# One block for setup and first attention of a two-layer decoder, with the loads and small products reordered

## What is computed

```python
q = (query @ w_q + b_q); k = (query @ w_k + b_k); v = (query @ w_v + b_v)     # 256 -> 16 * 128 each
weights = softmax(q k^T / sqrt(128), causal)
out = (weights @ v) @ w_o + b_o
Q, K = h @ Wq.T, h @ Wk.T                      # h is the context, 64 -> 64, 4 heads
sim = sum_heads(Q K^T) / 16                    # 256 x 256 per batch
threshold = 76th largest of each row of sim    # then sigmoid, mask, symmetric mean
```

## Time and profile before

| what | before |
|---|---|
| median of 3 runs, us | 876.88 (874.26 to 877.98) |
| the profiled execution, us | 877.31 |
| its span, us | 875.5 |
| TensorE busy | 793.7 us, 91% |
| VectorE, ScalarE, GpSimd busy | 65%, 48%, 57% |
| granted clock of TensorE, mean | 0.967 |

### The profile page before, as it was taken

One profiled execution on the slowest core, in us unless ns is written; L12 is line 12 of the kernel. 1 busy time (PEld: TensorE's weight loads), 2 busy tenths in 40 slices (PEclk: granted clock), 3 DMA queues, 4 the chain that ended last, 5 costly groups with the idle time before them and its releaser, 6 DMA issues. The chain is left out here.

```text
span 875.5 us, 14612 instructions
## 1 busy us (share of the span) xinstructions
PE 793.7 (91%) x4733; PEld 680.5 (78%) x4733; DVE 572.2 (65%) x1659; ACT 422.3 (48%) x1193; POOL 500.1 (57%) x409
## 2 busy tenths in 40 slices
PE   7889999999999976594899989999987799999995
PEld 5678888888988865293688878988885488888884
DVE  4696967868668576323678968777737655554555
ACT  5264635536346556061366654666663633323232
POOL 4857187566668451603475565367422386777763
PEclk9999999999999998797999999999999799999998
DMA  6220702204215211554210110110001011111111
GB/s 206 73 97 1 241 19 78 97 6 140 85 61 175 92 55 34 172 144 101 61 48 31 55 55 7 50 55 25 25 1 38 13 45 46 54 36 54 40 38 48
DMA packets 58331, 59.09 MB, mean 67 GB/s; under 512 B 5392, under 2 KB 49312, under 8 KB 58272
## 3 DMA queue, kind: packets, MB, share of 16 engines
q1 hardware_dynamic: 57504, 56.24, 20.7%
q0 software_dynamic: 768, 2.10, 0.7%
HBM read 50.00 MB, written 8.32 MB: 67 GB/s over the span
## 5 line engine op out<-in xcount | busy, mean ns | idle before, releaser
L981 ACT ACTIVATE a_probs<-bank,a_neg_peak 128x128 f32<-128x128 f32 (+1 forms) x256 | 103.5, 428 | 105.7 <-DVE a_neg_peak L1099 105.7
L1099 DVE CUSTOM_DVE_ANT_0 bank<-bank,causal 128x128 f32<-128x128 f32 (+1 forms) x256 | 82.7, 393 | 33.4 <-PE bank L842 32.1
L1009 ACT ACTIVATE a_probs<-a_probs,a_row_inv 128x128 f32<-128x128 f32 (+1 forms) x256 | 92.0, 454 | 8.3 <-DVE a_row_inv L1107 8.3
L987 ACT ACTIVATE a_probs_t<-bank 128x512 f32<-128x512 f32 x96 | 54.1, 600 | 62.3 <-PE bank L862 62.3
L881 PE MATMUL bank<-a_probs_t,a_vals 128*128 128x256 f32 x256 | 77.8, 386 | 3.3 <-DVE a_ot_lo L1119 3.3
L1821 POOL TENSOR_TENSOR d_h_lo<-d_h,d_h_hi 128x512 fp32r<-128x512 f32 x40 | 51.7, 1293 | 45.5 <-ACT d_h_hi L1941 31.9
L693 POOL TENSOR_TENSOR a_queries<-sim 128x512 f32<-128x512 f32 x32 | 41.1, 1283 | 62.2 <-DVE sim L1074 62.2
L2027 DVE TENSOR_TENSOR d_h<-d_silu,bank 128x512 f32<-128x512 f32 x40 | 27.5, 689 | 71.8 <-PE bank L128 70.5
L126 PE MATMUL bank<-a_wo_hi,a_ot_hi 128*128 128x256 f32 x256 | 73.0, 285 | 1.0 <-issue 1.0
L128 PE MATMUL bank<-a_wo_hi,a_ot_lo 128*128 128x256 f32 x256 | 72.0, 281 | 0.0
L127 PE MATMUL bank<-a_wo_lo,a_ot_hi 128*128 128x256 f32 x256 | 71.9, 281 | 0.0
(11 more groups left out here) (328 smaller groups left out, 2416.6 us busy)
## 6 DMA issues: line engine op xcount, KB each, us to landing
d_raw<-in_L_ffn_we_dram SPq DMA_DIRECT2D x48, 128.0 KB, 2.2
raw_k<-in_L_attn_w_k_dram SPq DMA_DIRECT2D x8, 512.0 KB, 6.8
raw_q<-in_L_attn_w_q_dram SPq DMA_DIRECT2D x8, 512.0 KB, 5.9
raw_v<-in_L_attn_w_v_dram SPq DMA_DIRECT2D x8, 512.0 KB, 7.9
raw_o<-in_L_attn_w_o_dram SPq DMA_DIRECT2D x8, 512.0 KB, 3.6
kv<-_L_ffn_expert_masks_dram SPq DMA_DIRECT2D x16, 256.0 KB, 3.0
kvt<-_L_ffn_expert_masks_dram SPq DMA_DIRECT2D x16, 256.0 KB, 3.2
raw_o<-in_L_attn_Wo_dram SPq DMA_DIRECT2D x8, 512.0 KB, 3.6
```

What stands on the lines that cost most here:

```text
L981: nc.scalar.activation(probs[s % 2][:, i, at:at + width], c.banks[i][:, at:at + width], ACT.Exp, bias=neg_peak[:, n:n + 1], scale=-1.0, ac ...
L987: nc.scalar.activation(probs_t[:, i * BANK:(i + 1) * BANK], c.banks[3 + (3 * s + i) % 2][:], ACT.Copy).then_inc(s_pt_free, 1)
L1009: last = nc.scalar.activation(part, part, ACT.Copy, scale=row_inv[:, s % 2, n + r:n + r + 1])
L1099: last = nc.vector.tensor_tensor_reduce(part, part, mask, -1.0, 3e38, ALU.add, ALU.min, neg_peak[:, n + r:n + r + 1])
```

## The change

`setup` goes, and a class `Beginning` takes its place; its parts are called from inside layer 0's attention block, so that there is one block in place of two. Raw keys and queries are loaded right after the first half of x, then biases, context, small weights, router, the second half of x, values. TensorE transposes the first half of x, runs four more warming matmuls into bank 7, transposes the biases, projects keys of step 0 (with a semaphore of their own, `s_split_k`), then transposes the context, small weights and the second half of x, projects the queries, and makes the context products and graph scores; the columns' products follow the scores of step 0. The doubled copies go from GpSimd to VectorE. Context and graph buffers live in buffers used later. GpSimd adds the output bias inside step 0, after the split of the second values; the wait for it at line 1194 goes, and one is written under `if rope and s == PASS_STEPS - 2`. What is not shown of the diff: the new semaphores and small buffers, and the copies and subtractions for high and low parts, which are those of before with their own semaphores.

```diff
...
-        with AttentionWeights(c, 0) as weights:
-            setup(c, weights)
-            attention(c, 0, weights)
+        with AttentionWeights(c, 0) as weights, Beginning(c) as beginning:
+            attention(c, 0, weights, beginning)
...
-def setup(c, weights):
...
+class Beginning:
...
+        self.ctx_nat = c.spare[:, 0].rearrange("p (t a d) -> p t a d", t=NT, a=2)
+        self.ctxt_hi, self.ctxt_lo, self.kt_hi, self.kt_lo = c.kvt_hi, c.kvt_lo, c.kvg_hi, c.kvg_lo
+        self.qt = c.kv_hi[:].rearrange("p t n -> p (t n)")
...
+    def loads(self, sp, weights):
+        c, a = self.c, self.a
+        sp.dma_start(c.ident[:], a["ident"]).then_inc(self.s_const, 16)
+        self.load_x(sp, 0)
+        for n in "kq":
+            weights.load(sp, n, 0)
+        for i, n in enumerate(("b_q", "b_k", "b_v")):
+            sp.dma_start(self.bias_nat[i * HEADS:(i + 1) * HEADS], a[f"L0_attn_{n}"].rearrange("(h d) -> h d", d=DH)).then_inc(self.s_bias, 16)
+        sp.dma_start(self.ctx_nat[:, :, 0], a["ctx_512"].rearrange("b (t p) d -> p (b t) d", p=P)).then_inc(self.s_ctx, 16)
+        for i, n in enumerate(("L0_xattn_Wq", "L0_xattn_Wk", "L1_xattn_W_k")):
+            sp.dma_start(self.w_nat[:, i, 0], a[n]).then_inc(self.s_w, 16)
+        sp.dma_start(self.r_nat[:], a["L0_ffn_router_w"]).then_inc(self.s_router, 16)
+        self.load_x(sp, 1)
+        weights.load(sp, "v", 0)
+        sp.dma_start(self.causal_f[:], a["causal"]).then_inc(self.s_mask, 16)
+        sp.dma_start(self.g_raw[:], a["L0_xattn_gamma_raw"].partition_broadcast(P)).then_inc(self.s_mask, 16)
+        sp.dma_start(c.rows[:, ROW_BK, 0:DC], a["L1_xattn_b_k"].partition_broadcast(P)).then_inc(self.s_key_bias, 16)
+        sp.dma_start(c.rows[:, ROW_BK, DC:P], a["L1_xattn_b_k"].partition_broadcast(P)).then_inc(self.s_key_bias, 16)
+        weights.load(sp, "o", 0)
+        sp.dma_start(c.ffn_weight[:], a["L0_ffn_weight"].rearrange("(k p) i -> p k i", p=P)).then_inc(c.s_ffn_weight, 16)
+        for r, n in ((ROW_BO, "L0_attn_b_o"), (ROW_SCALE, "L0_ffn_scale"), (ROW_GAMMA, "L1_xattn_ln_gamma"), (ROW_BETA, "L1_xattn_ln_beta")):
+            sp.dma_start(c.rows[:, r], a[n].partition_broadcast(P)).then_inc(c.s_rows, 16)
+    def load_x(self, sp, h):
+        sp.dma_start(self.c.x[:, 4 * h:4 * h + 4], self.a["x"][2 * h:2 * h + 2].rearrange("b (t p) d -> p (b t) d", p=P)).then_inc(self.s_x[h], 16)
+    def turn_x(self, pe, h):
+        c = self.c
+        pe.wait_ge(self.s_x[h], 16)
+        for k in range(KC):
+            for t in range(4):
+                last = self.nc.tensor.transpose(c.banks[3 + k][:, t * P:(t + 1) * P], c.x[:, 4 * h + t, k * P:(k + 1) * P], c.ident[:])
+            last.then_inc(self.s_x_t, 1)
+    def turn_first(self, pe):
+        c, nc = self.c, self.nc
+        pe.wait_ge(self.s_idle, 1)
+        keep_warm(c, 9)
+        pe.wait_ge(self.s_const, 16)
+        self.turn_x(pe, 0)
+        keep_warm(c, 4, 7)
+        pe.wait_ge(self.s_bias, 3 * 16)
+        nc.tensor.transpose(c.banks[2][:, 192:192 + 3 * HEADS], self.bias_nat[:], c.ident[0:3 * HEADS, 0:3 * HEADS]).then_inc(self.s_bias_t, 1)
+        pe.wait_ge(self.s_x_lo, KC)
+    def turn_others(self, pe):
+        c, nc = self.c, self.nc
+        pe.wait_ge(self.s_twice, 1)
+        for h in range(2):
+            for t in range(4):
+                last = nc.tensor.transpose(c.banks[h][:, t * P:(t + 1) * P], self.ctx_nat[:, 4 * h + t].rearrange("p a d -> p (a d)"), c.ident[:])
+            last.then_inc(self.s_ctx_t, 1)
+        pe.wait_ge(self.s_twice, 2)
+        pe.wait_ge(self.s_biased, 1)
+        for i in range(3):
+            nc.tensor.transpose(c.banks[2][:, i * DC:(i + 1) * DC], self.w_nat[:, i].rearrange("p a d -> p (a d)"), c.ident[0:DC, 0:DC])
+        pe.wait_ge(self.s_router, 16)
+        for k in range(KC):
+            last = nc.tensor.transpose(c.banks[2][:, 256 + k * EXPERTS0:256 + (k + 1) * EXPERTS0], self.r_nat[:, k * P:(k + 1) * P],
+                                       c.ident[0:EXPERTS0, 0:EXPERTS0])
+        last.then_inc(self.s_small_t, 1)
+        self.turn_x(pe, 1)
...
+    def products(self, pe):
+        c, nc = self.c, self.nc
+        pe.wait_ge(self.s_small_lo, 1)
+        pe.wait_ge(self.s_ctx_lo, 2)
+        for n in range(4):
+            if n == 3:
+                pe.wait_ge(self.s_x_lo, 2 * KC)
...
+        for h in range(2):
+            if h:
+                pe.wait_ge(self.s_qk_lo, 1)
...
+            last.then_inc(self.s_rows, 1)
+        pe.wait_ge(self.s_qk_lo, 4)
+        for b in range(B):
+            if b == 3:
+                pe.wait_ge(self.s_kv, 1)
...
+            last.then_inc(self.s_scores, 1)
+        pe.wait_ge(self.s_kv, 2)
+        pe.wait_ge(self.s_sim, 2)
+    def columns(self, pe):
+        for h in range(2):
+            pe.wait_ge(self.s_sim, 3 + h)
+            mm_stacked(self.nc, self.c.banks[3 + h][:], self.weight(2), self.ctxt_hi[:, cols], self.ctxt_lo[:, cols], False).then_inc(self.s_columns, 1)
...
+    def high(self, act):
+        c, nc = self.c, self.nc
+        self.high_x(act, 0)
+        act.wait_ge(self.s_bias_t, 1)
...
+        self.high_x(act, 1)
+        nc.scalar.activation(c.ident_bf[:], c.ident[:], ACT.Copy)
+        act.wait_ge(self.s_mask, 32)
+        nc.scalar.activation(c.causal[:, 1], self.causal_f[:], ACT.Copy)
+        nc.scalar.activation(self.g_exp[:], self.g_raw[:], ACT.Exp, scale=-1.0).then_inc(self.s_gamma, 1)
+        for n in range(4):
+            act.wait_ge(self.s_qk, n + 1)
+            nc.scalar.activation((self.qt, self.kt_hi)[n // 2][:, self.half(n % 2)], c.banks[n][:], ACT.Copy).then_inc(self.s_qk_hi, 1)
+        for b in range(B):
...
+    def low_first(self, dve):
+        c, nc = self.c, self.nc
...
+        self.low_x(dve, 0)
+        dve.wait_ge(self.s_ctx, 16)
+        nc.vector.tensor_copy(self.ctx_nat[:, :, 1], self.ctx_nat[:, :, 0]).then_inc(self.s_twice, 1)
+        dve.wait_ge(self.s_w, 3 * 16)
+        nc.vector.tensor_copy(self.w_nat[:, :, 1], self.w_nat[:, :, 0]).then_inc(self.s_twice, 1)
+        dve.wait_ge(self.s_biased, 1)
+    def low_others(self, dve):
+        c, nc = self.c, self.nc
+        for h in range(2):
+            dve.wait_ge(self.s_ctx_hi, h + 1)
...
+        dve.wait_ge(self.s_small_hi, 1)
...
+        self.low_x(dve, 1)
...
+    def gamma(self, dve):
+        c, nc = self.c, self.nc
+        dve.wait_ge(self.s_gamma, 1)
...
+        dve.wait_ge(self.s_sim, B)
+    def splits(self, pool, weights):
+        self.nc.gpsimd.memset(self.c.half_neg[:], -0.5)
+        self.nc.gpsimd.memset(self.c.one[:], 1.0)
+        pool.drain()
+        weights.first_splits(pool)
...
@@ -457,7 +512,7 @@
         parts = []
         for n, heads in (("k", min(self.KH, 2)), ("q", 2)):
-            if parts and self.rope:
+            if parts and (self.rope or s == 0):
                 self.split(pool, parts, self.s_split_k)
                 parts = []
...
@@ -646,6 +701,8 @@
                 if rope:
                     weights.load(sp, "q", 1)
                     weights.load(sp, "k", 1)
+                else:
+                    beginning.loads(sp, weights)
...
@@ -744,14 +801,12 @@
                 if rope:
                     rotate(0)
                 else:
+                    beginning.splits(pool, weights)
                     split_v(0)
                 split_proj(2)
                 if rope:
                     rotate(1)
                     weights.gather(pool, 1)
-                else:
-                    pool.wait_ge(c.s_rows, 4 * 16)
-                    nc.gpsimd.tensor_tensor(c.x[:], c.x[:], c.rows[:, ROW_BO].unsqueeze(1).broadcast_to([P, NT, D]), ALU.add).then_inc(s_residual, 1)
                 for s in range(LAST + 1):
                     if not rope and s % STEPS:
                         split_o(s // STEPS)
@@ -765,6 +820,9 @@
                         split_o(s // STEPS)
                     if s % STEPS == 0 and s < LAST - 1 and not rope:
                         split_v(s // STEPS + 1)
+                    if not rope and s == 0:
+                        pool.wait_ge(c.s_rows, 4 * 16)
+                        nc.gpsimd.tensor_tensor(c.x[:], c.x[:], c.rows[:, ROW_BO].unsqueeze(1).broadcast_to([P, NT, D]), ALU.add).then_inc(s_residual, 1)
                     if rope and s == NORM_STEP - 1:
                         weights.root(pool, 1)
                     if not rope and s % STEPS and s // STEPS < 4:
@@ -792,6 +850,8 @@
                         what, j = units(s)[u]
                         if rope and what == "k":
                             pe.wait_ge(weights.s_split_k, group_of(s, what) + 1)
+                        elif what == "k" and s == 0:
+                            pe.wait_ge(weights.s_split_k, 1)
                         else:
                             pe.wait_ge(s_split_proj, s + 1)
                         bank = claim("proj", s, u)
...
-                proj(0, range(len(units(0))))
                 if rope:
```

(25 more changed lines are left out.)

285 lines of the change are left out of this document (102 added, 183 removed).

## The result

| what | before | after |
|---|---|---|
| median of 11 runs each, us | 877.45 (874.26 to 880.3) | 871.45 (867.87 to 874.15) |
| the profiled execution, its span | 877.31, 875.5 | 867.87, 866.0 |
| granted clock, mean | 0.967 | 0.970 |

The ratio is 0.993, 95% interval 0.9912 to 0.9947: 6.0 us faster, 0.7% (4.7 to 7.7 us by the interval). The forecast was 870.3 with 867.5 to 874.5. It went by a median of 876.88 for before, from three runs; over eleven it is 877.45.

A forecast was written before the change was run, and what follows sets the result against it. TensorE, busy without a gap from 66 to 290 us, was taken as the bound, so gains lay ahead of it: 4.3 us in the front plus 2.3 in the search, 6.6 off, giving 870.3 us (range 867.5 to 874.5).

The forecast's parts named there:

- Part 1: Start of the front: with reordered loads, keys land at 6.7 us, biases at 8.9, and TensorE's first projection starts at 9.3.
- Part 2: First projection to step 1: 17.6 us of work plus 0.3 wait, step 1 at 27.2 against 31.47, 4.3 us won.
- Part 3: Top-k search: copy of sim no longer held by GpSimd's addition, first values at 33.1 us, 6.6 us won by then.
- Late and colliding (B): Rival, chance 0.15: late keys, longer graph-score wait, addition colliding with VectorE's search end or next copy; 3.3 us won, 873.6.
- Part 4: After the search: moved addition delays no loads, step 4's split ready about 65 us with 14 us slack, new wait costs nothing.
- The sum: Whole kernel: 4.3 + 2.3 = 6.6 us off, giving 870.3 us in terms of the median of before.
- A: Rival, chance 0.2: TensorE's clock falls in the wait before the keys, first projections lose 1.4 us; 5.2 won, 871.7.
- C: Rival, chance 0.1: the front was covered, something unseen takes the gain back after 290 us; 876 to 877.
- D: Rival, chance 0.05: pauses between small pieces keep TensorE at 1.2 GHz from 9.3 us until step 1; 11 us slower, 887.9.

## Why the prediction was right

- **Part 1** held. The first projection came at 9.67 against 9.3. Keys landed at 7.1 instead of 6.7 and the biases at 9.3 instead of 8.9; the clock stayed up behind the wait for the biases in both profiles of after (1.86 and 2.50 us).
- **Part 2** held: 17.70 us from there to step 1 against 17.6 + 0.3. The wait of the graph scores was 0.23 us. Together 4.1 us won against 4.3. That took the clock at 1.00 from 9.67 on, as the profiles of after show it; nothing says in how many of the eleven executions it was so.
- **Part 3** held, but for one line. First values 32.96 (33.1), search end 43.28 (43.5), 6.80 us earlier against 6.6. What it rests on, the addition holding the copy, is now shown by taking the copy away in before: 2.58 us. The line that failed is that GpSimd has nothing in flight at the first copy: its split of queries was (29.22 to 30.52), and the copy took 0.96 us instead of 0.3. That cost nothing, as the search's later operations waited for ScalarE's copy of the values in the run without the copy (0.85 us, up to 35.32) and came at the same time in after (35.34). The Trainium skill, "SBUF — State Buffer", section "Who interferes with whom", says that a VectorE instruction with at most one input in SBUF, outside the modes that take both port pairs, does not contend with GpSimd. The trace agrees with it for the maximum: at 35.53 in before without the copy, inside the addition, it took 0.43 us.
- **The step that was off** is in "Late and colliding (B)", from which the sum took nothing: "the next tile's copy has 1.6 us to spare before its results are wanted". It has none. The copy I put at about 47 came at 46.69, the addition at 43.12, as foreseen; the hold of 0.92 us went through VectorE's list, which has no wait for another engine there, and with the idle stretch at 62.57 it took back 1.21 us of what was won, between the transposes of step 0 (6.80) and the scores of step 3 (5.59). I had read the slack from who next reads the copy's result, and not from what is queued behind it on VectorE, which TensorE waits for.
- **Part 4**: the split for step 4 ended at 64.3 (65 foreseen), no wait for split weights came, and the wait in the branch that layer 0 never enters cost nothing.
- **The sum**: 6.6 less the 1.21 us that were taken back would be 5.4; the larger gain of the search (0.2 us) and 0.3 us won in steps 4 to 15 make it 5.9, and the medians say 6.0. The miss in time is 1.15 us, 871.45 instead of 870.3: 0.6 us are the gain (6.0 instead of 6.6), and the other 0.57 us the median of before, which moved from 876.88 to 877.45 with more runs. That the number came so near is in part luck of these sizes.
- **The rivals.** A (low clock) did not come in either profile of after, but it is open: the same front with four warming matmuls had the low clock in other runs, for 1.5 to 1.6 us, once in two profiles of one and the same kernel. The three profiles with the old front all show it, so a part of the gain may be a low clock that comes less often. B came in one of its terms, the next tile's copy. C and D did not come: 5.9 us are still there at 292 us, and no stretch after 17 us ran low in the front of after.

## What to carry to other kernels

An instruction's slack is that of the whole queue behind it: before putting a hold at nothing, follow the engine's list to the next place where another engine waits for it. Parts of a change that shift work in time don't add: here each of two gave 1.4 us alone and both together 5.6 (by the traces, at step 3), because making one engine earlier moved its copy under the other's long instruction, and the wait that followed brought the low clock. Where two engines get in each other's way, look first at whether the instruction that is held is needed at all; leaving out the copy removed every wait of TensorE for a held copy, and then it hardly mattered where the addition stood.

## What the runs showed of the hardware

- VectorE's copy of 128x256 from SBUF to SBUF waited for GpSimd's instruction in flight and took 0.28 to 4.67 us; all 28 copies that took over 0.3 us (before 290 us, nine profiles) ended 0.14 to 0.17 us behind that instruction, whether it was the addition or a split (37.55 and 37.40 in before, 52.35 and 52.19 with the addition in front), and two of them had been asked for only 0.02 and 0.07 us behind its start. The maximum and the replacement over the same data, with the same addition in flight, kept to 0.43 and 0.41 us.
- TensorE's clock behind a short wait differs between executions. Behind four warming matmuls and the wait for the biases it stayed at 1.00 (2.4 GHz) in five profiles, with waits of 1.86, 2.35, 2.50, 2.60 and 2.67 us, and fell to 0.50 (1.2 GHz) for 3 us or more in four, whose waits were no longer (1.72, 1.99, 2.03 and 2.20 us). Without the four it fell within the wait of 3.19 us, between 8 and 8.5 us; with nine and a wait of 1.44 us it stayed up, in one profile each. Farther on, a wait of 2.56 us was followed by 3.4 us at the low level (36.05 us, addition back in front). With six to twelve runs a kernel this can blur differences of a microsecond.
